# Sixteen images through four layers: the steady order of steps laid out anew, and two PSUM banks for the first image's transposes

## The chip, the cores and the metric

The kernel runs on one core of one Trainium2 chip. A core has five engines with an instruction stream each: TensorE (PE in the rows; its weight loads are PEld), VectorE (DVE), ScalarE (ACT), GpSimd (POOL) and SyncE (SP, which here only issues DMAs). They meet through semaphores alone. The metric is the device time of one execution in microseconds; before the change the median of 3 runs is 5643.53 us (5635.43 to 5649.11).

## The reference

The input x is 16 images of 64 x 64 pixels with 256 channels, in float32. Four layers follow, each `x = x + layer(group_norm(x))`:

```
layer 0: nearest of 1024 codes by distance, its code vector        (16 x 4096 pixels x 1024 codes)
layer 1: f, g, h = x Wf, x Wg, x Wh;  sigmoid(f g^T) h  per image row of 64 pixels
layer 2: x0, x1, x2 = three projections;  sm = softmax over n of x0[n] x1[m];
         gate[m] = sigmoid(sum_n x2[n] sm[n, m]);  out = gate * x    (4096 x 4096 exps an image)
layer 3: linear attention with 4 heads of 32 (softmax of q over d, of k over pixels),
         output product 128 -> 256, layer norm
```

The group norm takes its statistics over a whole image, so no layer of an image can start before the layer ahead of it has ended for that image.

## The kernel before

An image lies transposed in SBUF (tile XT, channels on partitions) in 8 groups of 512 pixels; a tile is 128 pixels, 32 an image. Two images are held. Work is cut into named steps; each engine has a function for its part of a step (`fill`, `exp`, `sums`, `score`, ...), whose waits on semaphores are inside, and runs its steps in an order that is written out by hand as a long list of calls. That list has three parts: a prologue (image 0 alone), a loop over images 1 to 15 (15 rounds, the steady order), and an epilogue. A round works on three images: `new` goes through layers 0 and 1 and the projections of layer 2, `old` through the 4096 x 4096 part of layer 2 and layer 3, and `last` through the end of layer 3 and out. An engine never passes a waiting step, so the order decides who idles. The steps named below are:

- `turn_in(im, c)`: TensorE transposes half a group of the input (4 transposes, L1213) into PSUM bank 7; VectorE copies it to XT (L839) and after each second one takes the group's statistics (L833). SyncE loads groups three ahead.
- `gn(im, layer, part)`: the statistics are put together over channels: DVE, PE (L1198), DVE, PE (L1201), DVE, POOL (power -0.5, L384), DVE.
- `l0_norm(im, g, part)`: ACT scales a group (parts 0 and 1, n_x, L504) and rounds it to half precision (parts 2 and 3, n_hi, L520); POOL makes the remainder n_lo (L392). `score` (PE, L1179, 6 products of 128 x 512) multiplies it with the codes, `best` and `index` (DVE) find the nearest, POOL gathers it, `turn0` (PE) transposes it back.
- `fill(im, h, z)`: two PE products with 12 rows each (L1347), into PSUM banks 2z and 2z+1; `exp(im, h, z)`: ACT's exp of those 1024 columns (L576), 128 an image; `sums(im, h)`: four PE products with 4 columns each (L1356) that add up both halves z. A fill waits until the exp of the half before it has read its banks.
- Layer 1: `l1_norm` (ACT L504, L534; POOL L409), `l1_fg`, `l1_h`, `l1_scores`, `l1_out` (PE L1256, L1179, L1280, L1290) and ACT's `l1_fg` (L543) and `l1_tanh` (L549, L553). All `l1_fg` and `l1_scores` share bank 4, so group g+1 can't be written before tanh(g) has read. `gated` (ACT L504 into xin or o_x), `gating` (DVE) and `gated_add` (POOL) belong to layer 2 of `old` and run among them, as does `spread` (PE).
- Layer 3: `l3_k`, `l3_qv`, `l3_kturn`, `l3_qturn`, `l3_ctx`, `l3_qsoft_`, `combine`, `final_z`, `final_out`. `project`, `columns`, `extremes`, `pieces` and `piece_turn` prepare layer 2 of `new`: the projections are turned, their extremes taken (DVE), cut into three pieces each (POOL L435 to L448) and turned (PE L1331).

The calls quoted here are the parts of TensorE's and ScalarE's lists that the prediction speaks of:

```
fill(old, 30, 0); sums(old, 28)
gn(new, 0, 1); fill(old, 30, 1); fill(old, 31, 0); gn(new, 0, 2); fill(old, 31, 1)
fill(old, 32, 0); sums(old, 29); sums(old, 30); sums(old, 31)
fill(old, 32, 1); fill(old, 33, 0); sums(old, 32)
```

Of the kernel before, what the change touches and what calls it, by code (L numbers as in the profile page):

```python
# [13 lines left out]
P = 128  # L14
KC = 2
# [3 lines left out]
NG = 8  # L19
# [13 lines left out]
XS = 3  # L33
# [51 lines left out]
def build(nc, x, emb, emb_t, wfg, bfg, wh, bh, w3, b3, wqv, wk, w_out, b_out, gamma, beta, ident_in, gmat_in, out):  # L85
# [4 lines left out]
    with ExitStack() as ctx:  # L90
# [137 lines left out]
        a_turned, a_kept = step("a_turned", 2 * NG, 2 * XS), step("a_kept", 2 * NG, 1)  # L228
# [147 lines left out]
        def _(pool):  # L376
# [96 lines left out]
            for new, old, last in images(B):  # L473
                final_sq(last, 1); final_sq(last, 3); final_sq(last, 5); final_sq(last, 7); final_sq(last, 9)
                final_sq(last, 11); final_sq(last, 13); final_sq(last, 15); gn(new, 0, 2); l0_norm(new, 0, 3)
                l0_norm(new, 1, 3); index(new, 0); index(new, 1); index(new, 2); index(new, 3); index(new, 4)
                l0_norm(new, 2, 3); index(new, 5); l0_norm(new, 3, 3); index(new, 6); index(new, 7); index(new, 8)
                index(new, 9); index(new, 10); index(new, 11); l0_norm(new, 4, 3); index(new, 12); index(new, 13)
                index(new, 14); index(new, 15); l0_norm(new, 5, 3); index(new, 16); index(new, 17); index(new, 18)
                index(new, 19); l0_norm(new, 6, 3); index(new, 20); index(new, 21); l0_norm(new, 7, 3)  # L480
                index(new, 22); index(new, 23); index(new, 24); index(new, 25); index(new, 26); index(new, 27)
                index(new, 28); index(new, 29); index(new, 30); index(new, 31); gn(new, 1, 2); l1_norm(new, 0)
                l1_norm(new, 1); gated_add(old, 0); gated_add(old, 1); l1_norm(new, 2); l1_norm(new, 3)
                gated_add(old, 2); gated_add(old, 3); l1_norm(new, 4); gated_add(old, 4); gated_add(old, 5)
# [13 lines left out]
        def _(act):  # L498
# [1244 lines left out]
```

## Time and profile before

| | |
|---|---|
| median of 3 runs | 5643.53 us |
| profiled execution | 5627.42 us, span 5625.5 us |
| mean granted TensorE clock | 0.966 |
| busy: PE, DVE, ACT, POOL | 5257.4, 4119.8, 3973.7, 1925.4 us |
| share of the span | 93%, 73%, 71%, 34% |
| HBM read, written | 136.78 MB, 67.11 MB |

The span runs from the first to the last instruction. An engine counts as busy while an instruction of its own runs, but a busy PE is not PE at its peak. The granted clock is TensorE's: 1.0 is 2.4 GHz, 0.5 is 1.2 GHz. In a row of the timeline stand the start, the duration of the merged instructions, the engine, the line, the operation with what it writes and reads, and in brackets how long the engine was idle before it and what ended that.

### The profile page before, as it was taken

What the parts mean: (1) busy time and instruction counts of PE and PEld (TensorE: products, weight loads), DVE (VectorE), ACT (ScalarE), POOL (GpSimd) and SP (SyncE); (2) the same over time, 40 slices, a digit from 0 to 9 for tenths busy, and PEclk for the clock granted to TensorE, in tenths of its full rate; (3) what the DMA queues carried; (4) which work ended last, traced back from release to release, by engine and by line L of the source; (5) the groups of instructions that cost most, each with busy time, mean ns of one, the idle gap of its engine ahead of it and who ended that gap; (6) DMA issues with size and microseconds to landing.
All of it is one profiled execution on the core that took longest, in us unless ns stands there. A gap on an engine that the chain in (4) does not pass through costs nothing.

```text
span 5625.5 us, 113928 instructions
## 1 busy us (share of the span) xinstructions
PE 5257.4 (93%) x44520; PEld 2742.7 (49%) x44520; DVE 4119.8 (73%) x8686; ACT 3973.7 (71%) x6017; POOL 1925.4 (34%) x1588
## 2 busy tenths in 40 slices
PE   7799999999999999999999999999999999999986
PEld 3435446363553645446364553645446364453624
DVE  8467677777777777677777777777777777777725
ACT  1467868677785877868677785877868677776793
POOL 2224243342423424243341423424243252423412
PEclk9899999999999999999999999999999999999996
DMA  2010201102011020201102011020201102011000
GB/s 81 9 38 13 66 26 40 46 7 71 21 61 31 13 66 15 65 27 39 47 7 70 22 61 31 13 66 14 64 28 36 47 11 69 23 57 34 3 31 31
DMA packets 163252, 211.22 MB, mean 38 GB/s; under 512 B 13216, under 2 KB 146080, under 8 KB 162720
## 3 DMA queue, kind: packets, MB, share of 16 engines
q1 hardware_dynamic: 138144, 136.79, 7.6%
q0 software_dynamic: 24576, 67.14, 4.1%
q8 instruction: 357, 5.85, 0.4%
q14 instruction: 175, 1.43, 0.1%
HBM read 136.78 MB, written 67.11 MB: 36 GB/s over the span
## 4 chain that ended last, share of the span: by engine, by line
PE 66%; ACT 13%; DVE 11%; issue 6%; POOL 2%; DMA 1%; ACTq 0%; DVEq 0%; POOLq 0%; SPq 0%
PE PS L1179 33%; PE PS L1356 15%; PE PS L1347 6%; ACT n_x L504 3%; DVE stats L833 2%; PE PS L1451 2%; PE PS L1213 2%; PE PS L1237 2%; PE PS L1290 2%; ACT big L576 2%; ACT xin L504 2%; ACT work L543 1%; ACT soft L576 1%; ACT attn L553 1%; ACT o_x L504 1%
## 5 line engine op out<-in xcount | busy, mean ns | idle before, releaser
L576 ACT ACTIVATE big<-PS 128x1024 f32<-128x1024 f32 x1376 | 1365.3, 1024 | 454.9 <-PE PS L1347 393.4
L576 ACT ACTIVATE soft<-PS 128x1024 f32<-128x1024 f32 x672 | 675.9, 1024 | 349.7 <-PE PS L1347 342.2
L399 POOL DMA_INDIRECT quant_H<-emb_t,idx x512 | 487.4, 952 | 980.0 <-DVE idx L857 788.1
L1179 PE MATMUL PS<-e_hi,n_hi 128*128 128x512 f16 x2048 | 781.4, 382 | 17.6 <-POOL n_lo L392 8.5
L1179 PE MATMUL PS<-e_lo,n_hi 128*128 128x512 f16 x2048 | 778.0, 380 | 0.0
L1179 PE MATMUL PS<-e_hi,n_lo 128*128 128x512 f16 x2048 | 777.7, 380 | 0.0
L1356 PE MATMUL PS<-big,w 128*4 128x512 f32 x5504 | 750.1, 633 | 0.0
L833 DVE BATCH_NORM_STATS2 stats<-XT 128x6 f32<-128x512 f32 x1024 | 651.8, 684 | 14.4 <-POOL XT L415 4.7
L857 DVE FIND_INDEX8 idx<-m,work 128x8 uint32<-128x1024 f32 x512 | 622.5, 1220 | 0.0
L1347 PE MATMUL PS<-rhs,lhs 12*128 12x512 bf16 x4096 | 556.0, 393 | 62.2 <-ACT big L576 38.7
L851 DVE CUSTOM_DVE_ANT_0 work<-PS,e_bias,m 128x512 f32<-128x512 f32 x512 | 384.2, 750 | 211.7 <-PE PS L1179 205.8
L851 DVE CUSTOM_DVE_ANT_0 work<-PS,e_bias 128x512 f32<-128x512 f32 x512 | 349.4, 683 | 248.6 <-PE PS L1179 247.1
L457 POOL TENSOR_TENSOR rstd<-rstd,mhalf 128x4 f32<-128x4 f32 x128 | 129.2, 1009 | 1118.8 <-DVE rstd L1038 1118.8
L1347 PEld LDWEIGHTS PS<-rhs,lhs 12*128 12x128 bf16 x4096 | 142.4, 91 | 714.0 <-ACT big L576 332.2
L504 ACT ACTIVATE n_x<-XT,gt,gs 128x512 f32<-128x512 f32 x512 | 391.8, 805 | 42.2 <-DVE gt L828 39.7
L392 POOL TENSOR_TENSOR n_lo<-n_x,n_hi 128x1024 f16<-128x1024 f32 x128 | 273.2, 2134 | 399.4 <-ACT n_hi L520 396.1
L1356 PE MATMUL PS<-soft,w 128*4 128x512 f32 x2688 | 376.9, 634 | 17.1 <-ACT soft L576 17.1
L1179 PEld LDWEIGHTS PS<-e_hi,n_hi 128*128 128x128 f16 x2048 | 199.7, 98 | 316.4 <-issue 70.9
L409 POOL TENSOR_TENSOR n_lo<-n_x,n_hi 128x1024 f16<-128x1024 f32 x128 | 273.3, 2135 | 207.4 <-ACT n_hi L534 154.5
L1049 DVE SCALAR_TENSOR_TENSOR yout<-soft,rstd,PS 128x256 f32<-128x256 f32 x512 | 222.2, 475 | 148.7 <-PE PS L1451 130.7
L415 POOL TENSOR_TENSOR XT<-XT,big 128x1024 f32<-128x1024 f32 x128 | 300.4, 2368 | 89.8 <-DVE big L945 89.8
L1179 PEld LDWEIGHTS PS<-e_hi,n_lo 128*128 128x128 f16 x2048 | 200.8, 98 | 242.9 <-issue 1.9
(208 smaller groups left out, 10817.4 us busy)
## 6 DMA issues: line engine op xcount, KB each, us to landing
xin<-x SPq DMA_DIRECT2D x128, 512.0 KB, 3.9
out<-yout SPq DMA_DIRECT2D x128, 512.0 KB, 2.9
quant_H<-emb_t,idx POOLq DMA_INDIRECT x512, 2.8
XT<-emb SPq DMA_DIRECT2D x1, 1024.0 KB, 6.0
XT<-wh SPq DMA_DIRECT2D x1, 256.0 KB, 5.7
XT<-wqv SPq DMA_DIRECT2D x1, 256.0 KB, 5.8
XT<-wk SPq DMA_DIRECT2D x1, 128.0 KB, 5.7
w_sb<-w SPq DMA_DIRECT2D x1, 128.0 KB, 5.4
```

The lines of the kernel that those rows point to most:

```text
L392: nc.gpsimd.tensor_tensor(n_lo[:, g % 2, :, :], n_x[:, g % 2, :, :], n_hi[:, g % 2, :, :], ALU.subtract).then_inc(l0_lo.sem, 1)
L399: nc.gpsimd.indirect_dma_start(quant[:, g % 2, u, :], None, emb_t, bass.IndirectOffsetOnAxis(ap=idx[:, t % (2 * GT), 0:1], axis=0),).then_ ...
L409: nc.gpsimd.tensor_tensor(n_lo[:, g % 2, :, :], n_x[:, g % 2, :, :], n_hi[:, g % 2, :, :], ALU.subtract).then_inc(l1_lo.sem, 1)
L415: nc.gpsimd.tensor_tensor(here, here, gated[:, g % 2, :, :], ALU.add).then_inc(g_added.sem, 1)
L504: return nc.scalar.activation(dst, XT[:, im % 2, k, g, :], copy, scale=gs[:, layer, k:k + 1], bias=gt[:, layer, k:k + 1])
L576: nc.scalar.activation(E[h % 3][:, z * 1024:(z + 1) * 1024], bank(2 * z, 2), ACT.Exp).then_inc(exped.sem, 1)
L833: last = v.bn_stats(stats[:, layer, k, g, :], XT[:, im % 2, k, g, :])
L851: v.tensor_tensor_reduce(biased[:, t % 2, part], bank(5 + half), e_bias[:, part], 1.0, m8[:, t % 2, 0:1] if half else -BIG, ALU.add, ALU.m ...
L857: v.max_index(idx[:, t % (2 * GT), :], m8[:, t % 2, :], biased[:, t % 2, :]).then_inc(l0_indexed.sem, 1)
L1179: ins = mm(dst, a, b, start=first and j == 0, stop=last and j == 2)
L1347: ins = mm(bank(r), lhs[rr, t * P:(t + 1) * P], rhs[rr, f * GW:(f + 1) * GW], start=True, stop=True)
L1356: ins = mm(PS[32 * q:32 * q + 4, 4, :], w2[:, t, f, :], E[h % 3][:, q * 512:(q + 1) * 512], start=h == 0, stop=h == HALVES - 1, skip_group ...
```

## The change

Two things change. First, the transposes of image 0 alone go to banks 7 and 3 in turn, and TensorE may be two half-groups ahead of VectorE's copy instead of one:

```diff
-        a_turned, a_kept = step("a_turned", 2 * NG, 2 * XS), step("a_kept", 2 * NG, 1)
+        a_turned, a_kept = step("a_turned", 2 * NG, 2 * XS), step("a_kept", 2 * NG, 2)
+        def turn_bank(im, c):
+            return 3 if im == 0 and c % 2 == 1 else 7
-                pe.wait_ge(*a_kept.room(im, c, 1))
+                pe.wait_ge(*a_kept.room(im, c, 2 if im == 0 else 1))
-                        ins = tr(PS[:, 7, (2 * k + u) * P:(2 * k + u + 1) * P],
+                        ins = tr(PS[:, turn_bank(im, c), (2 * k + u) * P:(2 * k + u + 1) * P],
-                v.tensor_copy(XT[:, im % 2, :, g, cols], bank(7).rearrange("p (k n) -> p k n", k=KC)).then_inc(a_kept.sem, 1)
+                v.tensor_copy(XT[:, im % 2, :, g, cols], bank(turn_bank(im, c)).rearrange("p (k n) -> p k n", k=KC)).then_inc(a_kept.sem, 1)
```

Second, the steady order of the loop is written anew on four engines (SyncE's stays, and so do prologue and epilogue). No step is added or dropped (the new `prepare` calls do nothing for images after the first). One line of each kind:

```diff
@@ TensorE
-                gn(new, 0, 1); fill(old, 30, 1); fill(old, 31, 0); gn(new, 0, 2); fill(old, 31, 1)
-                fill(old, 32, 0); sums(old, 29)
+                gn(new, 0, 1); fill(old, 31, 0); gn(new, 0, 2); fill(old, 31, 1); fill(old, 32, 0)
+                fill(old, 32, 1); sums(old, 29)
...
@@ VectorE
-                project(new); l3_q(old, 2); l3_qsoft_(old, 1); l3_k(old, 3); l3_ctx(old, 0); l3_kturn(old, 2)
-                l3_qturn(old, 0); columns(new); extremes(new)
+                project(new); l3_k(old, 3); l3_q(old, 2); l3_ctx(old, 0); l3_qsoft_(old, 1); l3_qsoft_(old, 2)
+                l3_qturn(old, 0); columns(new); extremes(new)
```

What it does to the instructions at two places of the round with image 7 new and 6 old. The first is TensorE from the first product of layer 0's statistics (`gn`) to the first score; `vv,gmat` is the second product, `rhs,lhs` are fills, `big,w` and `soft,w` sums, `e_hi,n_hi` a score. Before:

```order
L1198 MATMUL PS<-dm,gmat 128x2
L1347 MATMUL PS<-rhs,lhs 128x512 x4
L1201 MATMUL PS<-vv,gmat 128x2
L1347 MATMUL PS<-rhs,lhs 128x512 x4
L1356 MATMUL PS<-soft,w 4x512 x4
L1356 MATMUL PS<-big,w 4x512 x8
L1347 MATMUL PS<-rhs,lhs 128x512 x4
L1356 MATMUL PS<-soft,w 4x512 x4
L1347 MATMUL PS<-rhs,lhs 128x512 x4
L1179 MATMUL PS<-e_hi,n_hi 128x512
```

And now (the lines of the file are four further on here):

```order
L1202 MATMUL PS<-dm,gmat 128x2
L1351 MATMUL PS<-rhs,lhs 128x512 x2
L1205 MATMUL PS<-vv,gmat 128x2
L1351 MATMUL PS<-rhs,lhs 128x512 x6
L1360 MATMUL PS<-soft,w 4x512 x4
L1360 MATMUL PS<-big,w 4x512 x8
L1351 MATMUL PS<-rhs,lhs 128x512 x4
L1360 MATMUL PS<-soft,w 4x512 x4
L1183 MATMUL PS<-e_hi,n_hi 128x512
```

One half of a fill has moved ahead of the first product and one (32,1) from behind the sums 29 to 31 to their front; between the sums 32 and the first score no fill is left.

The second place is ScalarE in layer 1, from the end of `l1_norm(2)`: `work<-PS` alone and `attn` are `l1_tanh`, `work<-PS,fg_bias` is `l1_fg`, `n_x` and `n_hi` are `l1_norm`, `xin` and `o_x` are `gated`. Before:

```order
L504 ACTIVATE o_x<-XT,gt,gs 128x512 x2
L549 ACTIVATE work<-PS 128x256
L553 ACTIVATE attn<-work,ones 64x4x64 x2
L543 ACTIVATE work<-PS,fg_bias 64x256 x2
L504 ACTIVATE n_x<-XT,gt,gs 128x512 x2
L534 ACTIVATE n_hi<-n_x 128x1024
L549 ACTIVATE work<-PS 128x256
L553 ACTIVATE attn<-work,ones 64x4x64 x2
L504 ACTIVATE xin<-XT,gt,gs 128x512 x2
L504 ACTIVATE o_x<-XT,gt,gs 128x512 x2
L543 ACTIVATE work<-PS,fg_bias 64x256 x2
```

And now (three lines further on):

```order
L552 ACTIVATE work<-PS 128x256
L556 ACTIVATE attn<-work,ones 64x4x64 x2
L507 ACTIVATE o_x<-XT,gt,gs 128x512 x2
L507 ACTIVATE xin<-XT,gt,gs 128x512 x2
L507 ACTIVATE n_x<-XT,gt,gs 128x512 x2
L537 ACTIVATE n_hi<-n_x 128x1024
L546 ACTIVATE work<-PS,fg_bias 64x256 x2
L552 ACTIVATE work<-PS 128x256
L556 ACTIVATE attn<-work,ones 64x4x64 x2
L546 ACTIVATE work<-PS,fg_bias 64x256 x2
L507 ACTIVATE o_x<-XT,gt,gs 128x512 x2
```

`l1_tanh(0)` has moved ahead of `gated(2)`, and between it and `l1_fg(1)` there now stand two `gated` and `l1_norm(3)`; `l1_fg(1)`, `l1_tanh(1)` and `l1_fg(2)` follow each other with nothing between them.

## Rows read from the trace of the kernel before

**Rows 1.** The page: busy time; the loads (KB each, median us to landing).

```profile
PE 5257.4 (93%) x44520; PEld 2742.7 (49%) x44520; DVE 4119.8 (73%) x8686; ACT 3973.7 (71%) x6017; POOL 1925.4 (34%) x1588
...
xin<-x SPq DMA_DIRECT2D x128, 512.0 KB, 3.9
```

**Rows 2.** Timeline of ACT: the copy of the gate's sums, images 0, 6 and 14.

```profile
478.76 0.60 ACT L586 ACTIVATE yout<-PS 128x512 f32<-128x512 f32 x1 [0.58 <-PE PS L1356]
...
2508.93 0.60 ACT L586 ACTIVATE yout<-PS 128x512 f32<-128x512 f32 x1 [0.81 <-PE PS L1356]
...
5217.98 0.60 ACT L586 ACTIVATE yout<-PS 128x512 f32<-128x512 f32 x1 [1.68 <-PE PS L1356]
```

**Rows 3.** Busy time by stretch of one round: length, busy us, clock, DMA share, GB/s.

```profile
2281.70:2292.00 10.30, 8.46 (x76) 2.73 (x76) 7.77 (x27) 9.54 (x13) 0.00 (x0) 0.83 0.42 119
...
2360.00:2371.30 11.30, 9.26 (x52) 2.00 (x52) 0.91 (x7) 8.81 (x11) 2.82 (x2) 0.70 0.01 2
2371.30:2492.20 120.90, 120.86 (x724) 48.90 (x720) 97.97 (x214) 67.46 (x80) 43.53 (x37) 1.00 0.12 34
...
2510.50:2561.10 50.60, 46.85 (x620) 39.52 (x620) 44.87 (x75) 45.94 (x75) 34.28 (x16) 1.00 0.01 2
```

**Rows 4.** Timeline of PE in the prologue, the input's transposes.

```profile
17.06 1.08 PE L1213 MATMUL PS<-ident,xin 128*128 128x128 f32 x4 [0.88 <-DVE XT L839]
...
40.58 1.08 PE L1213 MATMUL PS<-ident,xin 128*128 128x128 f32 x4 [0.88 <-DVE XT L839]
```

**Rows 5.** Timeline of DVE there: a copy after its wait.

```profile
18.19 0.69 DVE L839 COPY XT<-PS 128x512 f32<-128x512 f32 x1 [1.27 <-PE PS L1213]
```

**Rows 6.** Timeline of PE from layer 0's statistics to the scores.

```profile
2365.04 3.57 PE L1356 MATMUL PS<-big,w 128*4 128x512 f32 x16
2368.55 0.39 PE L1347 MATMUL PS<-rhs,lhs 12*128 12x512 bf16 x4
2370.05 1.04 PE L1356 MATMUL PS<-soft,w 128*4 128x512 f32 x8 [1.11 <-ACT soft L576]
2371.03 0.40 PE L1347 MATMUL PS<-rhs,lhs 12*128 12x512 bf16 x4
2371.35 0.39 PE L1179 MATMUL PS<-e_hi,n_hi 128*128 128x512 f16 x1
...
2373.52 0.38 PE L1179 MATMUL PS<-e_lo,n_hi 128*128 128x512 f16 x1
2373.74 0.38 PE L1179 MATMUL PS<-e_hi,n_lo 128*128 128x512 f16 x1
2374.05 0.48 PE L1347 MATMUL PS<-rhs,lhs 12*128 12x512 bf16 x4
```

**Rows 7.** Timeline of ACT there.

```profile
2363.57 1.52 ACT L504 ACTIVATE n_x<-XT,gt,gs 128x512 f32<-128x512 f32 x2
...
2366.31 1.14 ACT L520 ACTIVATE n_hi<-n_x 128x512 f16<-128x512 f32 x2
2368.97 1.02 ACT L576 ACTIVATE soft<-PS 128x1024 f32<-128x1024 f32 x1 [1.52 <-PE PS L1347]
```

**Rows 8.** Timeline of ACT in layer 1: l1_fg(1) of image 7.

```profile
2520.43 0.95 ACT L543 ACTIVATE work<-PS,fg_bias 64x256 f32<-64x256 f32 x2
```

**Rows 9.** Timeline of PE in layer 1: l1_scores(1), l1_h(6,0).

```profile
2522.89 0.68 PE L1280 MATMUL PS<-work 32*64 32x64 f32 x16
...
2551.59 0.27 PE L1179 MATMUL PS<-h_hi,n_hi 128*128 128x256 f16 x1 [1.26 <-DVE XT L879]
```

**Rows 10.** Timelines of DVE (l3_qsoft(1), then l3_k(3)) and PE (piece_turn(0)).

```profile
2585.87 0.68 DVE L959 TENSOR_REDUCE qsum<-soft 128x16 f32<-128x512 f32 x1
...
2587.55 0.68 DVE L954 TENSOR_REDUCE kneg<-PS 128x1 f32<-128x512 f32 x1
...
2600.03 0.62 PE L1331 MATMUL PS<-ident,n_lo 128*128 128x128 bf16 x8 [0.91 <-POOL work L448]
```

**Rows 11.** Busy time by stretch, as rows 3: where the clock is at half.

```profile
2361.60:2365.00 3.40, 2.77 (x12) 0.47 (x16) 0.32 (x2) 3.40 (x5) 0.70 (x1) 0.50 0.02 5
```

More of the change, by code:

```diff
@@ L695, in _ @@
+                exp(old, 51, 1); exp(old, 52, 0); l0_norm(new, 7, 2); gated(old, 0); l0_norm(new, 7, 3)
                 exp(old, 52, 1); exp(old, 53, 0); exp(old, 53, 1); exp(old, 54, 0); exp(old, 54, 1)
@@ L709, in _ @@
[L709 to L712 removed]
+                l1_norm(new, 1); gate_chain(old, 1); gated(old, 1); l1_fg(new, 0); l1_norm(new, 2)
+                l1_tanh(new, 0); gated(old, 2); gated(old, 3); l1_norm(new, 3); l1_fg(new, 1); l1_tanh(new, 1)
@@ L1500, in _ @@
-                final_out(last, 1); fill(old, 9, 0); fill(old, 9, 1); sums(old, 7)
-                turn_in(new, 0); final_z(last, 3); fill(old, 10, 0); fill(old, 10, 1); sums(old, 8)
-                final_out(last, 2); final_z(last, 4); fill(old, 11, 0); fill(old, 11, 1); turn_in(new, 1)
+                final_z(last, 2); fill(old, 8, 1); fill(old, 9, 0); sums(old, 7)
+                final_out(last, 1); fill(old, 9, 1); turn_in(new, 0); final_z(last, 3); fill(old, 10, 0)
+                fill(old, 10, 1); sums(old, 8)
@@ new lines, in _ @@
+                fill(old, 13, 0); fill(old, 13, 1); sums(old, 11)
+                sums(old, 12)
+                fill(old, 14, 0); final_z(last, 6); final_out(last, 4); fill(old, 14, 1); fill(old, 15, 0)
+                turn_in(new, 3); sums(old, 13)
+                fill(old, 15, 1); final_z(last, 7); final_out(last, 5); turn_in(new, 4); fill(old, 16, 0)
+                fill(old, 16, 1); sums(old, 14)
+                turn_in(new, 5); final_z(last, 8); final_out(last, 6); fill(old, 17, 0); fill(old, 17, 1)
@@ new lines, in _ @@
+                sums(old, 15)
+                final_z(last, 9); final_out(last, 7); fill(old, 18, 0); fill(old, 18, 1); sums(old, 16)
+                turn_in(new, 6); fill(old, 19, 0); final_z(last, 10); final_out(last, 8); turn_in(new, 7)
+                fill(old, 19, 1); fill(old, 20, 0); sums(old, 17)
+                final_z(last, 11); final_out(last, 9); fill(old, 20, 1); fill(old, 21, 0); prepare(new, 0)
+                sums(old, 18)
+                turn_in(new, 8); final_z(last, 12); fill(old, 21, 1); fill(old, 22, 0); final_out(last, 10)
@@ new lines, in _ @@
+                fill(old, 62, 0); sums(old, 61)
+                fill(old, 62, 1); gn(new, 1, 1); fill(old, 63, 0); gn(new, 1, 2); fill(old, 63, 1); sums(old, 62)
+                sums(old, 63)
+                gate_chain(old, 0); l1_fg(new, 0); l1_h(new, 0, 0); spread(old, 0); spread(old, 1)
+                l1_h(new, 0, 1); l1_scores(new, 0); l1_h(new, 1, 0); spread(old, 2); l1_h(new, 1, 1)
+                l1_out(new, 0); l1_fg(new, 1); spread(old, 3); l1_h(new, 2, 0); l1_scores(new, 1); l1_h(new, 2, 1)
```

333 lines of the change are left out of this document (157 added, 176 removed).

## The prediction

> **What bounds the kernel now.** I read the page first: TensorE (PE) is busy 93% of the span, VectorE (DVE) 73%, ScalarE (ACT) 71% [rows 1]. So work taken from another engine brings nothing unless PE waits for it. Then I looked for the kernel's period. The copy of the gate's sums (L586) comes once an image, at 478.76 and, 14 images later, at 5217.98 [rows 2]: 338.5 us a steady iteration. Since 15 iterations are steady, 1 us in an iteration is 15 us of the program.
>
> The third view was the busy time by stretch of one steady iteration (image 7 new, 6 old) [rows 3]. In the scores' stretch of 120.90 us PE is busy 120.86 us: nothing but fewer or cheaper PE instructions makes that shorter. PE is less than busy in the first 10.3 us (8.46), round the statistics of layer 0 (9.26 of 11.3, granted clock 0.70) and in layer 1 (46.85 of 50.6). ACT is busy 45.94 of those 50.6 us, so in layer 1 ACT's order decides. An order can win in these places alone; the timelines of them are the fourth view.
>
> **The prologue.** PE writes four transposes of an input half-group into bank 7 and may write the next only once DVE has copied that bank. The handovers take turns: the fourth transposes start at 17.06 and the sixteenth at 40.58 [rows 4], 23.52 us for 12, 1.96 us each. DVE idles 1.27 us before every second copy [rows 5]. With banks 7 and 3 in turn the next transposes run beside the copy, and DVE becomes the bound. A pair then costs 3.92 - 1.27 = 2.65 us of DVE (copy, copy, two statistics). Seven pairs carry that gap, so the last copy comes 7 x 1.27 = 8.9 us earlier. Two covers are needed. The loads: group g+3 is issued when group g is turned, and is wanted four turns further on, at least 5.3 us, against a median landing of 3.9 us (the page's part 6 [rows 1]). And the setup product of the codes stands behind the last turn on PE in both versions, so it moves along. All after it is tied to PE and DVE and not to a clock time, so 8.9 us are saved once; without the covers nothing is. Bounds: 0 and 8.9, since DVE's gap is all there is to win. I take 8.9.
>
> **The steady order, place by place**, each worked out by carrying the durations of the rows along the new order by hand.
>
> *Statistics of layer 0.* In before, ACT does two of its four l0_norm parts, then an exp, then the other two; the n_hi parts start at 2366.31 and end at 2367.45 [rows 7], and GpSimd's n_lo runs to 2369.71. PE meanwhile does sums(29) to sums(31) at half the clock, until 2368.55, and only then fill(32,1), so ACT's exp(32,1) starts at 2368.97 after 1.52 us of idling, and PE waits 1.11 us for it before sums(32) [rows 6, 7]. In the new order fill(32,1) stands ahead of those sums and the four l0_norm parts stand together. They take 1.52 + 1.14 us and start at about 2363.0 (fill(30,1) now stands ahead of sums(28), so the exps before them run some 0.6 us sooner): n_hi is ready at 2365.7, n_lo (2.12 us) at 2367.9. Exps (32,0) and (32,1) are done by 2367.8, under the three slow sums. PE then needs a pair of fills (0.32) and sums(32) (0.98) and can begin score(0,0) at 2368.5 + 1.3 = 2369.8, where before began at 2371.35. The pairs of fills from here to the last score are as many as before (25). Gain 1.5 us an iteration; bounds: 0 (if the exps are late by the 1.1 us again) and 4.0 (if the sums also ran at the full clock, 2.6 us for 5.2).
>
> *Switching the array.* Neighbouring fills of both halves run side by side (four matmuls in 0.32 us), and a fill alone costs the same 0.32. And the last product of a score starts 0.31 us before a fill, where products follow each other at 0.22 [rows 6]: 0.09 us for the change from the whole array to four rows of tiles. Counted in the step lists of one iteration: from final sums and outputs up to the statistics, 34 units of fills become 33 (-0.3 us); within the scores, changes from the whole array to fills go from 17 to 20 and those from the whole array to sums or out of sums from 12 to 14: 5 x 0.1 = +0.5 us, and there PE has no slack. A page speaks against the change here: by the Trainium skill's TensorEngine Tiling (Array Packing), Key Properties, changing the tiling mode drains TensorE. The trace agrees, with the 0.09 us above; the sum takes the row.
>
> *Start of the iteration.* l3_kturn(7) goes behind the first fills, but PE waits there for DVE's subtraction and for the first exps anyhow, and combine(1) waits for DVE's combine(0), whose order is unchanged. Nothing up to there. After it final_out(0) moves into the wait that final_z(1) had, about 0.2 us. With the unit of fills above that is -0.5; bounds 0 and -1.5, the 1.84 us that PE is not busy in the first 10.3 [rows 3] less what those two chains keep.
>
> *Layer 1.* With sums(61) done earlier, ACT can copy the accumulators without the 0.81 us that it waits at 2508.93 [rows 2]. PE has no use for it: l1_fg(0) waits for GpSimd's l1 n_lo. Then ACT's order turns against it. Before, l1_fg(1) follows l1_tanh(0) directly (2520.43) and PE's l1_scores(1) stands at 2522.89 without a wait [rows 8, 9]. Now gated(2), gated(3) and l1_norm(3) lie between: 1.5 + 1.5 + 2.6 = 5.6 us. ACT leaves tanh(0) at 2518.2, so fg(1) is done at 2524.75; PE, which has lost its two waits of 0.2 and 0.27 and left out nothing, stands at l1_scores(1) at 2522.85 and waits 1.9 us. Behind it on PE is the rest of layer 1 (l1_h(2,1) first), behind fg(1) on ACT come tanh(1) and fg(2), each needing PE's step in between: 0.7 and 0.6 us of ACT idling, in a stretch that ACT now fills to 45.94 of 50.6 us [rows 3]. Two things pay most of it back: the 0.8 us, and l1_fg(6) now fills the wait of 1.26 us before l1_h(6,0) [rows 9]. Carried on to the statistics of layer 3 I come out 0.45 us late. Bounds -0.8 and +1.9.
>
> *Layer 3.* PE no longer waits 0.42 us for q(0), but waits some 0.8 for gn(2,1), which moved ahead. The chain that counts is DVE's: columns, extremes, GpSimd's pieces, and the first piece_turn, for which PE waits 0.91 us already [rows 10]. DVE now does l3_qsoft(2) ahead of columns (from 2585.87 to 2587.55 one takes 1.7 us [rows 10]) and l3_kturn(2) (0.6) behind it; with 0.4 us of slack gained earlier, piece_turn(0) comes 0.65 us later. Bounds 0 and +1.1.
>
> Sum of an iteration: -1.5 + 0.5 - 0.5 + 0.45 + 0.65 = -0.4 us; times 15, -6 us. With the prologue -14.9, say -15. The epilogue's order is unchanged. The profiled execution took 5627.42 us (span 5625.5), which is 16.1 below the median of the three runs shown, 5643.53; the sum would make it 5612.4. For the median I subtract the same 15: 5628.5.
>
> **Rivals.**
> A, only the prologue counts: what is won at layer 0 is given back in full by layers 1 and 3 (their upper bounds, 1.9 + 1.1, are more than the 1.5). For it: PE waits again for l1_scores(1) and piece_turn(0). 5643.5 - 8.9 = 5634.6.
> B, the plan holds: layers 1 and 3 cost nothing (ACT idles there, but its waits fall where PE has other work), the 1.1 us come off the sum: -1.5 us an iteration, and -2.0 with the start's bound. 5643.5 - 8.9 - 15 x 2.0 = 5605. Against it: the fixed order on ACT, which leaves it nothing else to do.
> C, slower: the granted clock falls once or twice more. In before it stands at half (1.2 GHz) from 2361.60, after PE had waited for the statistics and for exps [rows 11]. The new waits (1.9 at l1_scores(1), a like one before l1_fg(6), 1.6 before piece_turn(0)) are as long as those, where there were shorter ones. That row is 3.4 us at a granted clock of 0.50, which is 1.7 us of work lost. It decides from one more fall an iteration, unhidden: -0.4 + 1.7 = +1.3, with two falls +3.0: 5643.5 - 8.9 + 20 to + 45 = 5654 to 5680.
> D, the falls go away. PE ran sums(29) to sums(31) at half the clock. Were it to stay at full rate, the bound of 4.0 us at layer 0 holds: -2.9 an iteration, 5643.5 - 8.9 - 43 = 5591. The Trainium skill's TensorE: Matmul & The Clock Gate, Part 1, has the halved clock as the idle state that activity ends; by that, less idling means fewer falls. The trace agrees in part only: PE had waits before the fall, but worked between them [rows 6]. In the new order PE still waits for exps (31,0) and (31,1) just there, about 1 us, so I give D little.
>
> **How the numbers follow.** Forecast 0.40, A 0.18, B 0.22, C 0.15, D 0.05. What a measurement of this kernel can tell from no change is about 0.2%, 11 us, so faster means below 5632 and slower above 5655. The forecast's own range is 5614 to 5643, and 0.7 of it lies below 5632 (0.28); with B and D and a quarter of A that is 0.60. Same: the rest of the forecast and of A, 0.25. Slower: C, 0.15. Range 5592 to 5657: it leaves out the better half of D and the worse part of C. The predicted time is 5628.
>
> **What would show it.** The prologue: the sixteenth turn near 31.7 us and DVE without the 1.27 us gaps. The period: L586's interval near 338.0 less 0.4. Layer 0: PE's wait before sums(32) gone, and score(0,0) some 1.5 us sooner after gn(0,2) (10.16 us in before). Layer 1: a PE wait for ACT's fg of near 2 us before l1_scores(1). Layer 3: a longer wait before piece_turn(0) than 0.91. I am wrong if the period falls by more than 1.5 us or rises, or if the granted clock is low in layer 1, where it is 1.00 before [rows 3].

## The result, and the profile after

The changed kernel takes 5758.0 us (median of 4 runs, 5755.6 to 5761.2), the kernel before 5639.5 us (4 runs, the three of the table above and one more): the ratio is 1.0211, 95% interval 1.0199 to 1.0224. The change makes the kernel 2.1% slower. The prediction said 5628 us, range 5592 to 5657.

The page of the changed kernel, whose span is 5753.7 us, against [rows 1]: TensorE is busy 98 us longer with the same 44520 instructions, at a mean granted clock of 0.945 where it was 0.966.

```profile
PE 5354.9 (93%) x44520; PEld 2773.8 (48%) x44520; DVE 4126.6 (72%) x8686; ACT 3972.8 (69%) x6017; POOL 1919.0 (33%) x1588
```

The timeline of ACT, the copy of the gate's sums for images 0, 4 and 14, against [rows 2]:

```profile
472.37 0.58 ACT L589 ACTIVATE yout<-PS 128x512 f32<-128x512 f32 x1
...
1860.74 0.58 ACT L589 ACTIVATE yout<-PS 128x512 f32<-128x512 f32 x1
...
5338.65 0.58 ACT L589 ACTIVATE yout<-PS 128x512 f32<-128x512 f32 x1
```

The first copy is 6.4 us earlier than the 478.76 of before, so the prologue did gain. From then on an iteration takes (5338.65 - 472.37) / 14 = 347.6 us where it took 338.5: 9.1 us more, 127 over the 14. Before has a few longer rounds in that mean; settled rounds are 337.9 and 347.9, 10.0 apart. The interval from image 14 to image 15 is another 7.5 us longer (261.3 for 253.8 us). -6.4 + 127.1 + 7.5 = 128.2 us is the whole difference of the two spans.

The next view is the busy time by stretch of one iteration, cut at the same ten steps of TensorE in both kernels. The columns are the stretch, its length, PE's busy time and instructions, PE's granted clock, DMA share and GB/s. Before, round 7 (image 7 new):

```profile
2282.68:2297.83 15.15, 13.46 (x114) 0.89 0.36 105
2297.83:2360.10 62.27, 61.81 (x509) 1.00 0.33 111
2360.10:2371.35 11.25, 9.30 (x52) 0.70 0.01 2
2371.35:2498.32 126.97, 126.93 (x773) 1.00 0.12 34
2498.32:2503.77 5.45, 3.33 (x24) 1.00 0.02 9
2503.77:2510.49 6.72, 5.74 (x32) 0.75 0.00 0
2510.49:2557.93 47.44, 43.97 (x586) 1.00 0.01 2
2557.93:2583.50 25.57, 24.82 (x239) 1.00 0.01 2
2583.50:2600.03 16.53, 14.75 (x207) 1.00 0.01 1
2600.03:2620.53 20.50, 19.60 (x259) 1.00 0.01 3
```

And the changed kernel, round 5:

```profile
1631.85:1651.81 19.96, 19.57 (x128) 0.66 0.23 79
1651.81:1712.78 60.97, 60.30 (x502) 1.00 0.36 113
1712.78:1722.89 10.11, 8.99 (x52) 0.66 0.00 0
1722.89:1850.93 128.04, 127.56 (x777) 1.00 0.11 33
1850.93:1856.49 5.56, 4.16 (x31) 1.00 0.04 15
1856.49:1863.20 6.71, 4.68 (x24) 0.64 0.01 4
1863.20:1914.97 51.77, 47.50 (x586) 0.92 0.01 1
1914.97:1942.21 27.24, 24.78 (x239) 1.00 0.01 2
1942.21:1958.91 16.70, 15.24 (x182) 1.00 0.01 2
1958.91:1979.72 20.81, 19.14 (x283) 1.00 0.01 2
```

The steps at the cuts are fill(0,0), final_z(1), gn(0,1), score(0,0), turn0(15), gn(1,2), l1_fg(0), gn(3,2), project, piece_turn(0) and the next fill(0,0). Length and clock are to be read together. Four places matter:

- The start: 4.8 us longer, granted clock 0.66 for 0.89. A mean of 0.66 over 20 us is about 13.7 us at half rate (1.2 GHz), where it was 3.4.
- The statistics of layer 0 are 1.1 us shorter at about the same clock, and the scores behind them 1.1 us longer at full clock (0.6 of it is busy time of PE, the rest waits).
- Layer 1 (l1_fg(0) to gn(3,2)): 4.3 us longer, clock 0.92 where it was 1.00.
- Layer 3 (the last three): 64.75 for 62.60 us, all at full clock.

Round 6 of the changed kernel separates the two causes without any edit. In its scores TensorE waited 2.54 us for a gather, everything behind came later, and its layer 1 ran at full clock; round 7's start then was only 6.8 us at half rate. Round 7's start and round 6's layer 1:

```profile
2215.49:2263.76 48.27, 43.42 (x587) 1.00 0.01 2
...
2328.51:2345.45 16.94, 16.75 (x128) 0.80 0.28 94
```

The same instructions in the same order take 48.27 or 51.77 us, and 16.94 or 19.96 us, depending on the clock. So of layer 1's 4.3 us, 0.8 are the order's and 3.5 the clock's. The start's own part comes out of the first group of experiments.

### The profile page after: what moved, and what is told of

It is laid out like the page before. It is cut to its first block, busy times and chain, and to the rows that moved or that the text cites. A ratio compares the mean times of both kernels' runs of the same rounds, so it can differ in the third digit from the quotient of the medians.

```text
span 5753.7 us, 113928 instructions
## 1 busy us (share of the span) xinstructions
PE 5354.9 (93%) x44520; PEld 2773.8 (48%) x44520; DVE 4126.6 (72%) x8686; ACT 3972.8 (69%) x6017; POOL 1919.0 (33%) x1588
## 4 chain that ended last, share of the span: by engine, by line
PE 66%; DVE 12%; ACT 11%; issue 7%; POOL 3%; DMA 1%; ACTq 0%; DVEq 0%; POOLq 0%; SPq 0%
PE PS L1183 32%; PE PS L1360 14%; PE PS L1351 6%; ACT big L579 2%; PE PS L1455 2%; DVE stats L836 2%; PE PS L1217 2%; PE PS L1241 2%; ACT n_x L507 2%; PE PS L1294 2%; DVE work L854 1%; DVE XT L882 1%; DVE idx L860 1%; ACT xin L507 1%; PE PS L1260 1%
## 5 line engine op out<-in xcount | busy, mean ns | idle before, releaser
L1351 PE MATMUL PS<-rhs,lhs 12*128 12x512 bf16 x4096 | 573.8, 403 | 54.5 <-ACT big L579 25.3
L412 POOL TENSOR_TENSOR n_lo<-n_x,n_hi 128x1024 f16<-128x1024 f32 x128 | 273.1, 2133 | 217.2 <-ACT n_hi L537 130.2
L1183 PE MATMUL PS<-h_hi,n_hi 128*128 128x256 f16 x1024 | 293.7, 287 | 15.7 <-DVE XT L882 11.8
```

The lines of the kernel that those rows point to most:

```text
L412: nc.gpsimd.tensor_tensor(n_lo[:, g % 2, :, :], n_x[:, g % 2, :, :], n_hi[:, g % 2, :, :], ALU.subtract).then_inc(l1_lo.sem, 1)
L1183: ins = mm(dst, a, b, start=first and j == 0, stop=last and j == 2)
L1351: ins = mm(bank(r), lhs[rr, t * P:(t + 1) * P], rhs[rr, f * GW:(f + 1) * GW], start=True, stop=True)
```

## The experiments

Many of these kernels stand between the two orders: an iteration's lists can be cut, on all engines at once, where the same steps have been done in both, and a region taken from the one or the other. Theory H says that the loss is TensorE at half rate, in stretches that follow its new waits (in the statistics of layer 1, in layer 1 and at the end of layer 3). Rival W says that the new order's own waits cost it and the clock only goes along. Rival S, of the first group, says that the order at the start brings its own half rate there.

**Bisection, and the clock held up.** The two banks alone have before's lists with the changed kernel's `turn_bank`.

> The order of before with the two banks alone. By both theories the prologue ends 6.4 us earlier (that is what the first copy of the gate's sums gained in the changed kernel's trace, 478.76 to 472.37 us) and the period stays at 338 us: 5639 - 6 = 5633 us, range 5628 to 5637. If the two banks had a part in the loss, it would be above 5640.

Measured: 5627.2 us against 5638.9, ratio 0.9978 (0.9968 to 0.9987). That is 1 us under the stated range. The prologue's part of the change is a gain of about 0.2%, with the first copy of the gate's sums at 470.4 us in the profile. The other kernels stand on this one.

> Two banks, and the new order only from the start of an iteration to the last score (start, statistics of layer 0, scores); the statistics of layer 1, layer 1 and layer 3 keep the order of before. Theory H (half rate): the new half-rate stretches start where TensorE has waited a little more, and those waits are in the statistics of layer 1, in layer 1 and at the end of layer 3; so this kernel keeps the three stretches of before (13.7 us an iteration) and gives 5610 to 5640 us. Rival W (the waits themselves, by the terms of the prediction): -1.5 + 0.5 - 0.5 an iteration, 5633 - 22 = 5611 us. Rival S (the order at the start causes its own 13.6 us at half rate): 5633 + 15 x 5 = 5708 us.

> Two banks, and the new order only in the statistics of layer 1, in layer 1 and in layer 3; start, layer 0 and scores keep the order of before. Theory H: half-rate stretches as in the changed kernel, 30 to 34 us an iteration, 5730 to 5765 us. Rival W: 0.45 + 0.65 us an iteration, 5633 + 17 = 5650 us. Rival S: half rate longer only after the scores, 5633 + 15 x 5 = 5700 us.

Measured: front 5664.2 us (1.0043, 1.0026 to 1.0060), back 5708.4 us (1.0123, 1.0106 to 1.0140). Against 5627 that is +37 and +81, nearly the whole loss of 131 between them. I had expected the front to be free, and of the back at least 5730: by H all of the new half rate comes with it. It has 27 us an iteration at half rate in most rounds, and its time is nearer to rival S's 5700. So part of the half rate comes with the front's order, and H in its first form is wrong about the places. The front's rounds are of two kinds; the start of round 7 and of round 9:

```profile
2291.04:2307.49 16.45, 15.65 (x127) 0.90 0.33 97
...
2966.68:2987.49 20.81, 20.71 (x128) 0.59 0.24 78
```

With 3.4 us at half rate, as before, this start and the stretch behind it (16.45 + 60.97) take 77.42 us, exactly before's 15.15 + 62.27. At equal time at half rate the new order at the start neither gains nor loses; it runs into more half rate.

The fourth kernel keeps the changed kernel's order and adds work in TensorE's waits:

```diff
+            def busy(im, b, n):
+                for j in range(n if 0 < im else 0):
+                    mm(bank(b), e_hi[:, 0, 0:P], e_hi[:, 0, 0:512], start=True, stop=True)
...
             def gate_chain(im, part):
+                busy(im, 2, 4)
                 pe.wait_ge(*acc_kept.after(im))
...
             def l1_fg(im, g):
+                if g == 6:
+                    busy(im, 3, 5)
                 pe.wait_ge(*l1_tanhed.room(im, g, 1))
```

> The changed kernel with 19 products of 128x512 more an iteration, whose result nobody reads, put where TensorE waits: before l3_qturn(5) 2, before the first fill 3, in the second part of layer 1's statistics 2, before the gate's turn 4, before l1_scores(1) 3, before l1_fg(6) 5. Each takes 0.22 us at the full clock. Theory H: they keep the clock up, the half-rate stretches shrink from 34 us an iteration towards the 13.7 of before, and the kernel gets faster with more work: 5640 to 5710 us. Rival W: the clock is a bystander; 5758 us where the products lie in waits, up to 5758 + 15 x 4.1 = 5820 us where they don't.

Measured: 5682.7 us (1.0078, 1.0061 to 1.0095), 75 us less than the changed kernel with 4.1 us more TensorE work an iteration. Mean clock 0.968. The start, the gate and layer 1 of its round 7:

```profile
2309.24:2326.53 17.29, 16.35 (x140) 0.90 0.28 92
...
2530.56:2537.72 7.16, 4.79 (x32) 1.00 0.00 0
2537.72:2585.99 48.27, 45.25 (x594) 1.00 0.01 2
```

Layer 1 is at the 48.27 us of the undisturbed round, in 12 of 13 rounds. W alone can't explain a kernel that gets faster by useless work: the half rate is a cause of the loss. It isn't the whole loss. This kernel is still 55 us above the one with two banks alone, and its round 10, with only 3.4 us at half rate where before has 13.7, takes 340.4 us, 2.6 more than before.

**Which region, and is it the place of the products?** Each of the next three has one region of the new order on the two-bank kernel. The edit of the first, its lines wrapped anew and cut (ahead of them `turn0(14)`, `turn0(15)` and sums(58) each change places with a half of a fill):

```diff
@@ TensorE, statistics of layer 1
-                fill(old, 62, 0); sums(old, 60); fill(old, 62, 1); fill(old, 63, 0); gn(new, 1, 1); gn(new, 1, 2)
-                fill(old, 63, 1); sums(old, 61); sums(old, 62)
+                sums(old, 60); fill(old, 62, 0); sums(old, 61); fill(old, 62, 1); gn(new, 1, 1); fill(old, 63, 0); gn(new, 1, 2)
+                fill(old, 63, 1); sums(old, 62)
```

> Two banks, order of before, and the new order on TensorE alone from turn0(14) to the statistics of layer 1 (sums 60 and 61 sooner, fill(63,0) between the two statistics products, fill(62,1) ahead of them). Theory H: this order leaves TensorE waiting 1.1 us for the copy of the gate's sums where it waited 0.7; its fall is followed by 10.2 us at half rate in place of 3.4 in most iterations: 5627 + 15 x 2.5 = 5665 us. Rival W: the wait moves and nothing is lost, 5620 to 5627 us.

> Two banks, order of before, and the new order of layer 1 alone (PE, ACT, DVE, GpSimd). Theory H: a new fall of 3.4 us before l1_h(6,0) in most iterations (1.3 us) and the 0.45 us of the prediction: 5627 + 15 x 1.7 = 5653 us. Rival W: 5627 + 15 x 0.45 = 5634 us.

> Two banks, order of before, and the new order of layer 3 alone (PE, ACT, DVE, GpSimd). Theory H: the wait of 0.6 us before l3_qturn(5) and of 0.8 us before the first fill come from here, so the start of the iteration runs 6.8 to 13.6 us at half rate where it ran 3.4: 5627 + 15 x 2.5 = 5665 us and more. Rival W: 5627 + 15 x 0.65 = 5637 us.

Measured: statistics of layer 1 5651.6 us (1.0023, 1.0013 to 1.0033), layer 1 5676.2 us (1.0069, 1.0052 to 1.0085), layer 3 5665.8 us (1.0048, 1.0031 to 1.0065). Each is slower than 5627 by more than W allows. They don't add up: 24, 49 and 39 us are 112, where the kernel with all three lost 81. Layer 1's is twice what I expected: at full clock (its round 3) its stretch takes 49.17 us for 47.44, so 1.7 us are real waiting, and the rest is half rate, in its own end and in the start of the next iteration. Layer 3's stretches take 27.24, 16.71 and 20.86 us at full clock, the changed kernel's 27.24, 16.70 and 20.81.

```diff
@@ the control, in place of all other products
             def score(im, t, half):
+                if half == 0 and 8 <= t < 17:
+                    busy(im, 5, 3 if t == 8 else 2)
```

> The changed kernel with only 6 of the unread products: 2 in layer 1's second statistics product, 4 before the gate's turn. Theory H, by stage: from l1_fg(0) to the second statistics product of layer 3 the changed kernel takes 51.7 us with 8.7 us at half rate, and 48.3 us in the one iteration without; this kernel is at 48.3 in nearly all of them, 3.4 us an iteration: 5758 - 50 = 5708 us (5695 to 5725), while the start of an iteration stays at 20 us with 13.7 at half rate. Rival W: 5758 us or up to 5778 us.

> The changed kernel with the same 19 unread products as in the run that held the clock, but all inside the scores (before the first half of scores 8 to 16), where TensorE has no wait. Theory H: they cover no wait, so no fall is prevented and 19 x 0.22 = 4.1 us an iteration are added, 5758 + 62 = 5820 us (5790 to 5830, since the iteration may fall into another pattern of half rate). If any product helped, wherever it stood, it would be under 5740 us.

Measured: with 6 products at the gate 5706.2 us (1.0117, 1.0100 to 1.0134), 52 us less; with 19 in the scores 5797.4 us (1.0294, 1.0263 to 1.0325), 39 us more. The gate, layer 1 and the start of the former:

```profile
1622.67:1642.62 19.95, 19.60 (x127) 0.66 0.26 80
...
1846.88:1854.05 7.17, 4.79 (x33) 1.00 0.00 1
1854.05:1902.32 48.27, 43.41 (x586) 1.00 0.01 2
```

Layer 1 is at 48.3 us in 9 of 13 rounds of the former, fewer than I had expected, and its start stays at 13.7 us or more at half rate in 11. The control has as many products as the kernel above that gained 75 us; only their place differs. They cost 3.6 us in the scores (131.5 for 127.9), 54 in 15 iterations. Two of its four executions ran at the changed kernel's mean clock (0.943 and 0.944) and took 5813.1 and 5812.2 us, 55 more than it; the other two had 0.953 and 0.951 and took 5772.1 and 5782.5. The profiled execution, the fastest of the four, had 23 us an iteration at half rate where the changed kernel has 32; that is why its loss is less than the 62 us of the forecast.

**What makes the fall at the start.**

> The changed kernel with the order of before from the first fill to turn_in(14) on PE, ACT and DVE. If the start's own order makes the 13.7 us at half rate there: 3.4 to 6.8 us remain, 5758 - 15 x 3 = 5713 us. If the waits at the end of layer 3 make it: 13.7 stay and the time is 5750 to 5765 us (start and the stretch behind it take 77.4 us in either order at the same half rate).

> The changed kernel with 5 unread products, 2 before l3_qturn(5) and 3 before the first fill. Theory H: the fall at the start goes in part of the iterations (13.7 to 3 or 7 us at half rate), and the one in layer 1 stays (51.7 us): 5758 - 15 x 2 = 5728 us, 5705 to 5745. Rival W: 5758 us, up to 5775.

> The changed kernel with the whole of layer 3 (PE, ACT, DVE, GpSimd) in the order of before. By stages, layer 3 itself goes from 64.8 us to 62.6 (27.24, 16.71, 20.81 to 25.57, 16.53, 20.50), all at full clock, 15 x 2.2 = 32 us: 5726 us if the half-rate stretches stay. Theory H: the waits of 0.6 and 0.8 us ahead of the first fill are gone too, and the start of an iteration has 3.4 or 6.8 us at half rate in most iterations where it had 13.7: up to 3 us more, 5680 to 5705 us. If the start's own order makes its fall: 5720 to 5730 us.

Measured: 5713.9 us (1.0133, 1.0116 to 1.0150), 5717.8 (1.0140, 1.0123 to 1.0157) and 5704.7 (1.0115, 1.0098 to 1.0132). With layer 3 as before, the start still ran 13.7 us or more at half rate in 11 of 13 rounds; with the start as before it ran 3.4 or 6.8 us in 10 of 13. Products in the waits ahead of it (0.6 and 0.8 us) keep it to 6.8 us or less in 8 of 13 rounds, where the changed kernel has 1. So it is the new order of the start that makes the long fall common, and layer 3's isn't needed for it. But that doesn't clear the waits: I had expected them to go with layer 3's new order, and the trace shows that they don't. `l3_kturn(7)` now stands behind the first fills, and in the kernel with layer 3 restored TensorE waits 1.17 us ahead of the first fill, in the changed kernel 0.82; with the start as before it waits 0.23 there (0.34 in the kernel before), and 0.72 two fills later. The first fills of the changed kernel, of the one with layer 3 restored and of the one with the old start:

```profile
1631.85 0.78 PE L1351 MATMUL PS<-rhs,lhs 12*128 12x512 bf16 x4 [0.82 <-DVE soft L982]
```

```profile
2319.81 0.78 PE L1349 MATMUL PS<-rhs,lhs 12*128 12x512 bf16 x4 [1.17 <-DVE soft L982]
```

```profile
3008.61 0.79 PE L1348 MATMUL PS<-rhs,lhs 12*128 12x512 bf16 x4 [0.23 <-DVE soft L982]
3010.11 0.61 PE L1348 MATMUL PS<-rhs,lhs 12*128 12x512 bf16 x2 [0.72 <-ACT big L579]
```

Whether that longer wait makes the long fall, or the work behind it, no run separates. Restoring layer 3 still gave 53 us, which by itself lies at the upper end of what I had forecast for the case that the start's fall goes: 32 by its own stretches (62.59 us again), the rest by less half rate in some rounds. The two starts in whole, old order and then layer 3 restored:

```profile
3008.61:3024.37 15.76, 14.47 (x114) 0.78 0.31 102
```

```profile
2319.81:2340.26 20.45, 19.71 (x128) 0.67 0.28 78
```

**Layer 3's own 2.15 us.** TensorE's waits there, changed kernel, round 5 (layer 2's first statistics product, l3_ctx(0), l3_qv(2)):

```profile
1929.15 0.38 PE L1202 MATMUL PS<-dm,gmat 128*128 128x2 f32 x2 [0.70 <-DVE dm L816]
1934.88 0.46 PE L1427 MATMUL PS<-xin,soft 128*32 128x32 f32 x32 [0.94 <-issue]
1937.84 0.28 PE L1183 MATMUL PS<-qv_hi,o_hi 128*128 128x256 f16 x1 [0.49 <-DVE soft L982]
```

What l3_ctx(0) waits for is DVE's copy of l3_kturn(0) (L973), which now stands behind the statistics. DVE there, and GpSimd at the same time:

```profile
1932.04 0.14 DVE L824 TENSOR_TENSOR dm<-dm,PS 128x2 f32<-128x2 f32 x1
1932.22 1.76 DVE L825 TENSOR_TENSOR vv<-dm 128x2 f32<-128x2 f32 x1
1934.09 0.69 DVE L973 COPY soft<-PS 128x512 f32<-128x512 f32 x1
```

```profile
1931.84 2.13 POOL L423 TENSOR_TENSOR o_lo<-o_x,o_hi 128x1024 f16<-128x1024 f32 x1 [7.66 <-ACT o_hi L611]
```

The squaring of 128x2 numbers takes 1.76 us. In the kernel before, the same instruction takes 0.16:

```profile
2578.97 0.16 DVE L822 TENSOR_TENSOR vv<-dm 128x2 f32<-128x2 f32 x1
```

In all 15 iterations of the changed kernel it is this long, and it ends with GpSimd's L423 to within 0.02 us; in none of before is it over 0.3 us. The new order moved it into GpSimd's work. The Trainium skill's SBUF — State Buffer (SBUF: two separate sides) says that a VectorE instruction with two SBUF inputs and a GpSimd instruction that reads SBUF exclude each other from a pair of ports, and whichever starts first keeps it for its whole length. The trace agrees, with 1.76 for 0.16 us behind a GpSimd instruction that had started 0.38 us earlier.

The test moves one step of DVE back:

```diff
-                ... l3_q(old, 0); l3_k(old, 1); gn(new, 2, 1); l3_kturn(old, 0); l3_qsoft_(old, 0)
+                ... l3_q(old, 0); l3_kturn(old, 0); l3_k(old, 1); gn(new, 2, 1); l3_qsoft_(old, 0)
```

> The changed kernel with one step of VectorE's layer 3 moved back: l3_kturn(0) ahead of l3_k(1), as before, and not behind the first statistics part of layer 2. In the changed kernel that copy comes 4.7 us after its transposes and TensorE waits 0.94 us for it before l3_ctx(0). If that copy is what costs layer 3: the stretch from layer 3's statistics to the projections goes from 27.2 to 26.3 us, and the time by 0 to 15 x 0.94 = 14 us: 5744 to 5758 us. If it is TensorE's own early gn(2,1): the stretch stays at 27.2 or the wait moves to the step behind it.

Measured: 5744.9 us (1.0191, 1.0174 to 1.0208), 13 us less. The stretch is 26.62 us, not 26.3: l3_ctx(0) no longer waits, but l3_qv(2) waits 0.89 us in place of 0.49 behind the instruction that is still held up.

```profile
1910.83:1937.45 26.62, 24.70 (x238) 1.00 0.01 2
```

**Can it be turned into a gain?**

```diff
@@ TensorE's list of before, with two banks
-                fill(old, 0, 1); fill(old, 1, 0); fill(old, 1, 1)
+                fill(old, 0, 1); busy(new, 6, 3); fill(old, 1, 0); busy(new, 6, 2); fill(old, 1, 1)
...
-                fill(old, 33, 0); sums(old, 32)
+                fill(old, 33, 0); busy(new, 5, 4); sums(old, 32)
```

> The order of before, two banks, and 18 products of 128x512 an iteration whose result nobody reads, in TensorE's waits: 1 before the first fill, 3 before fill(1,0), 2 before fill(1,1), 1 in layer 0's second statistics product, 1 before fill(31,1), 1 before fill(32,0), 4 before sums(32), 3 in layer 1's second statistics product, 3 before the gate's turn (19 counted singly, 4.1 us at full clock). Theory H: the 13.6 us an iteration at half rate in the order of before shrink to 0 to 7 us; at the 0.4 us per us that the intervals of the changed kernel show (341.0 us with 17.0 at half rate, 347.8 with 34.1) that is 2.5 to 5 us an iteration less the part of the products that the waits do not cover: 5570 to 5615 us. Rival W: 5627 us at best, up to 5627 + 62 us.

> Two banks, the new order only where its stretch was shorter (TensorE's and ScalarE's statistics of layer 0: 10.1 us for 11.3 with the same half rate; TensorE's statistics of layer 1: 46.7 for 47.4 us behind them), everything else as before, and 10 unread products: 1 in layer 0's second statistics product, 3 before fill(32,1), 2 in layer 1's second statistics product, 4 before the gate's turn. Theory H: 1.1 + 0.8 us by the order and 2 to 3 us by less half rate, 334 to 336 us an iteration: 5575 to 5600 us. Rival W: 1.9 us less 10 x 0.22 us of products, 5627 us.

Measured: 5614.6 us (0.9957, 0.9941 to 0.9974) and 5618.4 us (0.9967, 0.9954 to 0.9979). Both beat before. But both settled on 337.9 us an iteration, as before has, and the second missed H's range (5575 to 5600). The mixed kernel won 0.8 us in layer 1, and its start took on 6.8 us at half rate for 3.4, with 0.9 us more in the stretch behind. The kernels' settled rounds pile up at 337.9, 341.2, 344.7 and 347.9 us. Can a round have any other length? Theory S of the next run (steps, another S than above) says no.

> Two banks, the order of before, and 4 unread products (0.86 us) an iteration inside the scores, where TensorE has no wait. Three kernels with different work at a period of 337.9 us, and others at 341.2, 344.7 and 347.8, suggest that where the falls land lets an iteration settle on lengths some 3.4 us apart. Theory S (steps): the 0.86 us are either absorbed (5627 us, period 337.9) or cost a whole step (5627 + 15 x 3.4 = 5678 us). If times simply add: 5627 + 13 = 5640 us.

Measured: 5649.2 us (1.0021, 1.0012 to 1.0031), 22 us more than without the 4 products. Neither branch of theory S holds: the rounds alternate between 339.0 and 340.2 us. But times don't simply add either: 0.86 us of work cost 1.5 us a round.

> What the runs so far make the best of: two banks, the order of before, the new order only in TensorE's statistics of layer 1 (0.8 us shorter behind them at full clock), and 19 unread products: 1 before the first fill, 3 and 2 before fill(1,0) and fill(1,1), 1 in layer 0's second statistics product, 1, 1 and 4 before fill(31,1), fill(32,0) and sums(32), 2 in layer 1's second statistics product, 4 before the gate's turn. Added up from the stages at their least half rate: 15.5 + 62.3 + 10.2 + 127.0 + 5.0 + 7.2 + 46.6 + 25.6 + 16.6 + 20.0 = 336.0 us an iteration; 337.9 if the falls take it back, as in the two kernels before it: 5585 to 5615 us, 5590 likeliest.

> The same without the 6 unread products at the start of the iteration, which there took about as long as the fall that they prevent (35.5 us with them and none at half rate, 35.6 without and with 3.4). If stages add: the same time as its neighbour, within 5 us. If what decides is where the falls land: different by up to 2 us an iteration, 30 us, either way.

Measured: 5601.0 us (0.9935, 0.9918 to 0.9953) and 5610.9 us (0.9953, 0.9935 to 0.9970). The first is the fastest of all, 0.65% under before and 2.7% under the changed kernel, at a mean clock of 0.977. Its rounds lie between 335.9 and 339.3 us. The start, layer 0's statistics and the gate in round 7, the shortest; in most others the gate has no half rate, and layer 1 has 3.4 us of it and takes 48.3 us where round 7 takes 46.65:

```profile
2269.55:2285.07 15.52, 13.72 (x121) 1.00 0.31 103
...
2347.35:2357.60 10.25, 9.79 (x59) 0.83 0.01 2
...
2489.49:2496.66 7.17, 6.04 (x33) 0.76 0.00 0
```

Without the six products at the start the rounds settle on 337.8 us again, with 6.8 us at half rate there and none at layer 0 (9.37 us). The two medians are 10 us apart, and not within 5 as they would be if stages added. The profiled spans of the fastest and of before differ by only 21.5 us of the 39 of the medians. The profiled execution of before was itself 13 us under its median, so what the rest of the gain is made of, no trace here shows.

## Why the prediction was wrong

Settled rounds, us an iteration, from the two tables. `order` is the difference at equal time at half rate, `half rate` what is left:

```
step of the prediction     forecast   order   half rate   from
statistics of layer 0        -1.5     -1.1      0         11.25 -> 10.11
scores                       +0.5     +1.1      0         126.97 -> 128.04
before gn(1,2), gate          0       +0.1      0         5.45, 6.72 -> 5.56, 6.71
start                        -0.5      0.0     +3.5       77.42 -> 80.93; 77.42 at equal clock
layer 1                      +0.45    +0.8     +3.5       47.44 -> 51.77; 48.27 at clock 1.00
layer 3                      +0.65    +2.15     0         62.60 -> 64.75
sum                          -0.4     +3.0     +7.0       337.85 -> 347.87
```

**The prologue** was right in its mechanism. The pairs of turns run 2.51 us apart and DVE copies without its 1.27 us gaps:

```profile
27.22 1.81 PE L1217 MATMUL PS<-ident,xin 128*128 128x128 f32 x8 [0.57 <-DVE XT L842]
29.73 1.22 PE L1217 MATMUL PS<-ident,xin 128*128 128x128 f32 x8 [0.70 <-DVE XT L842]
```

The last two half-groups begin at 29.73 us, so the sixteenth is at about 30.3 where I said 31.7. That is 10.3 us earlier than the 40.58 of before [rows 4], more than my bound of 8.9, and the bound was too low: a pair now takes 1.41 us less (2.51 for 3.92) and not 1.27, and the fourth half-group already began 1.8 us sooner (15.27 for 17.06). By the first gate copy the gain was 8.4 us with the banks alone and 6.4 in the changed kernel.

**The step that failed most** is the sum itself. It had no term for the clock, and the clock cost 7.0 of the 10.0 us; it was rival C, with 0.15, whose 5654 to 5680 the time is also above. Both signs that I had named for being wrong came: the period rose, and the granted clock in layer 1 fell to 0.92. C named the mechanism, but missed it three ways. It priced a fall by one row of 3.4 us [rows 11], where the falls that came last 10.2 and 13.7 us. Even the fall of that row is longer, because its window ends inside it: the 3.4 us behind it are at half rate too. And the waits before it were not as long as the new ones, as I had written: the longest between those of the start and the fall is 0.32 us. The stretch behind that of rows 11:

```profile
2365.00:2368.40 3.40, 3.40 (x20) 0.44 (x12) 0.00 (x0) 2.15 (x4) 0.81 (x1) 0.50 0.01 2
```

C looked for them at l1_scores(1), l1_fg(6) and piece_turn(0), where I had found new waits. One came there, 3.4 us in most rounds, behind a wait of 1.81 us before l1_fg(6); the two long ones are at the start, where I had booked a gain of 0.5 and "nothing up to there" for l3_kturn(7) behind the first fills (TensorE waits 0.82 us ahead of them for 0.34), and at the gate's turn, where I wrote that "PE has no use for" ACT's earlier copy. And it took half of a fall as lost, where 10.3 us more at half rate at the start cost 3.5 us. Of the missing 1.6 us, 0.4 are TensorE's waits there, which shrank from 0.80 to 0.39; for the rest no run shows the reason.

At the gate the forecast was wrong in fact. Sums(61) had been PE's work between the second statistics product and the gate; moved ahead, it leaves PE waiting 1.18 us where it waited 0.72:

```profile
1861.38 1.11 PE L1369 MATMUL PS<-ident,yout 128*128 128x128 f32 x4 [1.18 <-ACT yout L589]
```

The stretch to l1_fg(0) is no longer for it (6.71 us), because l1_fg(0) waits for GpSimd in both kernels. That is why a count of waits shows nothing here: the idling is free where it is and paid for in layer 1, where most of the half rate is gone once products fill the wait at the gate.

**Layer 3** was mis-sized: +0.65 with an upper bound of 1.1, measured +2.15. The failing sentence is "The chain that counts is DVE's: columns, extremes, GpSimd's pieces". I had seen that PE would wait 0.8 us for gn(2,1), measured 0.70, and let it go as covered. It wasn't, and l3_ctx(0) and l3_qv(2) added 0.94 and 0.49, while the 0.42 for q(0) went: together 1.71 for the 1.67 us that the first of the three stretches lost. I had carried DVE's squaring along as 0.16 us into GpSimd's work; its 1.6 us more are longer than either wait, but a kernel without them wasn't run. The first piece_turn, which I thought would decide, waits less than before, 0.51 us for 0.91 [rows 10]; the other 0.48 us are in the last two stretches, where TensorE waits more ahead of l3_qturn(5) and of the first fill.

**Layer 1** went as worked out: ACT's l1_fg(1) stands behind l1_norm(3) and starts at 1878.18, and PE waits for it before l1_scores(1), 0.78 us in round 5 and 1.36 in round 6, for the 1.9 forecast; +0.8 for +0.45. That 0.8 is the sum of two: layer 1's own order lost 1.7 at full clock (49.17 for 47.44), and the order of the statistics ahead of it gained 0.8 (46.65 in the undisturbed rounds of the kernel that has it alone).

```profile
1879.17 0.68 PE L1284 MATMUL PS<-work 32*64 32x64 f32 x16 [0.78 <-ACT work L546]
```

**Layer 0 and the scores** had the right signs. The scores' 1.1 us are 0.6 of work, near the 0.5 for switching the array, and 0.4 of waits that the forecast did not have. PE's wait of 1.11 us before sums(32) [rows 6] is gone, as forecast, but a wait of 0.70 us for an exp stands before fill(32,1) and the three slow sums are still at half rate:

```profile
1715.70 0.60 PE L1351 MATMUL PS<-rhs,lhs 12*128 12x512 bf16 x2 [0.70 <-ACT big L579]
1716.23 1.89 PE L1360 MATMUL PS<-soft,w 128*4 128x512 f32 x8
1717.90 3.64 PE L1360 MATMUL PS<-big,w 128*4 128x512 f32 x16
```

**Rival D** named something real. In the last kernel, whose layer 0 has no half rate in its settled rounds, layer 0's statistics take 9.37 us instead of 11.25.

## What to carry to other kernels

When TensorE is the bound and its granted clock is under 1.00 anywhere in a steady loop, a reordering must be judged by the clock column of each stretch before any count of waits: the same instructions cost up to 3.5 us more or less here. A wait that costs nothing where it stands can be paid for later, and a few unread full-size products in it can bring more than they cost; a control with the same products elsewhere shows whether it is that. Small VectorE instructions with two SBUF inputs should not be moved beside long GpSimd ones without a look at their durations there.

## What was not expected of the hardware

- Half rate came behind short waits and went on under steady work. At the start of round 5 PE is busy 19.57 of 19.96 us and still has a granted clock of 0.66. Ahead of the fall it had waited 0.6 and 0.8 us. What it does there is fills (12 of 128 rows) and sums (4 columns); no fall began inside the scores, with their 128x128 weights, unless a gather was late. The Trainium skill's TensorE: Matmul & The Clock Gate (Part 1) has the half rate as the idle state and activity as its end. This trace agrees in that work put into the waits made the falls rarer, and differs in that stretch of 19.57 busy us. What ends a fall, and why it lasts 3.4 us in one round and 13.7 in another, no run here shows.
- The same wait can be followed by a fall or not. Before l1_fg(6) TensorE waits 1.81 us in round 5 and 1.82 in round 6 of the changed kernel; behind it come 3.4 us at half rate in round 5, none in round 6.
- A gain or loss of 1 us in an iteration does not come out as 1 us: 0.86 us of added work cost 1.5, and 0.8 us gained in layer 1 vanished in the mixed kernel. Many kernels settle on one of a few round lengths some 3.4 us apart, but one alternated between 339.0 and 340.2 us.
- One VectorE instruction of 128x2 took 1.76 us in place of 0.16 beside GpSimd's 2.13 us.
